# Second attention of a two-layer block: V as the stationary operand in 32-column windows, scores in two parts, loads issued a stage earlier

## The reference

```
q = (x @ wq).reshape(b, s, 32, 16)      # and k, v
q = rotary(q); k = rotary(k)
scores = einsum('bqhd,bkhd->bhqk', q, k) / 4
scores = where(causal, scores, min)
probs = softmax(scores)                 # over 256 keys
out = einsum('bhqk,bkhd->bqhd', probs, v).reshape(b, s, 512)
x = x + ga * (out @ wo)
# then: layernorm, base and router of the feed-forward, LoRA, sum
```

## Time and profile before

| | us |
|---|---|
| median of 3 runs | 2289.11 (2288.36 to 2294.61) |
| the profiled execution | 2288.56 |
| its span | 2286.5 |
| PE busy | 2075.5 (91%) |
| DVE busy | 1523.6 (67%) |
| ACT busy | 867.3 (38%) |
| POOL busy | 843.6 (37%) |

### The profile page before, as it was taken

How to read it: one execution, slowest core, us unless ns; L and a number is a source line. 1 busy time by engine, 2 the same in 40 slices (tenths; PEclk the granted TensorE clock), 3 DMA queues, 4 the chain that set the end, 5 groups by cost and what they waited for, 6 DMA issues and landing times. The chain is left out here.

```text
span 2286.5 us, 41946 instructions
## 1 busy us (share of the span) xinstructions
PE 2075.5 (91%) x13536; PEld 1830.8 (80%) x13536; DVE 1523.6 (67%) x2334; ACT 867.3 (38%) x2214; POOL 843.6 (37%) x789
## 2 busy tenths in 40 slices
PE   7789977999999999999999999669969999996873
PEld 3178867999999999999999999559958999995762
DVE  1446656787787787787787787478833444443885
ACT  1022223444444444444444444244523444433321
POOL 0012325444444444444444433258632222220224
PEclk9889998999999999999999999879988999997997
DMA  4546751111111111111111111236563222210003
GB/s 155 180 156 214 242 197 60 55 42 41 55 41 42 55 41 45 51 41 46 51 41 46 48 30 32 72 107 191 161 173 101 77 76 76 75 50 30 29 23 115
DMA packets 189217, 192.30 MB, mean 84 GB/s; under 512 B 18008, under 2 KB 167128, under 8 KB 188152
## 3 DMA queue, kind: packets, MB, share of 16 engines
q1 hardware_dynamic: 189176, 191.77, 26.9%
HBM read 120.33 MB, written 62.98 MB: 80 GB/s over the span
## 5 line engine op out<-in xcount | busy, mean ns | idle before, releaser
L836 PE MATMUL ps_q<-ht_hi,wq 128*128 (+1 forms) x2048 | 288.3, 284 | 18.2 <-DVE wq L759 18.2
L836 PEld LDWEIGHTS ps_q<-ht_hi,wq 128*128 128x128 f32 x2048 | 269.1, 192 | 23.6 <-DVE wq L759 18.4
L663 ACT ACTIVATE prob<-ps_s,neg_max 128x128 f32<-128x128 f32 (+1 forms) x512 | 208.6, 420 | 142.9 <-DVE neg_max L739 118.8
L798 POOL TENSOR_TENSOR q_rot<-q_rot,q_swap 128x512 f32<-128x512 f32 x128 | 165.4, 1292 | 197.9 <-DVE q_swap L732 197.9
L670 ACT ACTIVATE pt<-ps_s 128x512 fp32r<-128x512 f32 x192 | 108.2, 600 | 308.8 <-PE ps_s L887 308.8
L875 PE MATMUL ps_y<-wo,ot 128*128 (+1 forms) x780 | 198.1, 402 | 0.0
L875 PE MATMUL ps_o<-wo,ot 128*128 (+1 forms) x780 | 193.7, 397 | 0.2
L1690 POOL TENSOR_SCALAR_AFFINE_SELECT f_prob<-f_prob 128x512 f32<-128x512 f32 x128 | 81.6, 637 | 281.5 <-ACT f_prob L1672 281.5
L1741 PE MATMUL f_ps_o<-values,f_prob 128*128 (+1 forms) x1536 | 182.8, 276 | 0.7 <-DVE o L1645 0.7
L1741 PEld LDWEIGHTS f_ps_o<-values,f_prob 128*128 128x128 f32 x1536 | 178.8, 193 | 0.9 <-issue 0.9
L793 POOL TENSOR_TENSOR prob<-prob,inv_sum 128x512 f32<-128x512 f32 x64 | 66.7, 1042 | 296.2 <-DVE inv_sum L748 296.2
(11 more groups left out here) (235 smaller groups left out, 4490.8 us busy)
## 6 DMA issues: line engine op xcount, KB each, us to landing
stack_dram<-e_part SPq DMA_DIRECT2D x192, 128.0 KB, 2.3
v_dram<-v_part SPq DMA_DIRECT2D x32, 512.0 KB, 5.9
k_dram<-k_part SPq DMA_DIRECT2D x64, 256.0 KB, 2.7
kk<-k_dram SPq DMA_DIRECT2D x128, 128.0 KB, 2.1
vv<-v_dram SPq DMA_DIRECT2D x128, 128.0 KB, 2.1
wmod<-in_wmod SPq DMA_DIRECT2D x12, 1024.0 KB, 5.5
f_q<-stack_dram SPq DMA_DIRECT2D x64, 192.0 KB, 2.6
f_k<-stack_dram SPq DMA_DIRECT2D x128, 96.0 KB, 2.5
```

The costliest lines, as they stand in the source:

```text
L663: nc.scalar.activation(p[:, h], sc[:, h], ACT.Exp, bias=neg_max[:, t, h:h + 1], accum_out=row_sum[:, t, h:h + 1]).then_inc(p_exp, 1)
L798: nc.gpsimd.tensor_tensor(qrot[j][:], qrot[j][:], qswap[j][:], ALU.add).then_inc(q_add, 1)
L836: mm = nc.tensor.matmul(ps_q[j][:, e], w[:, c:c + HD0], r[:, bass.ds(u % B, 1), k].rearrange("p o s -> p (o s)"), start=(n == 0), stop=(n ...
```

## The change

**Attention.** V is loaded from memory as `f_v` tiles for two units: for each unit, key tile and head a window of 32 columns, in which the 16 columns of V stand at 0 to 15 or 16 to 31, by the unit's parity, and zeros elsewhere. The window is the stationary operand and P streams (`values`, line 1798 now). Head h writes partitions 32h to 32h+31; two units fill one tile of [128, 2, 256]: the products, and beside them the sums, made by the same products with `ones` as stationary operand. Everything is accumulated in one group over both units. The result has features on the partitions, so nothing is turned in the router stage; the rows of wo are permuted on the host to fit. DVE takes one reciprocal and one product for two units, behind the maxima. The scores are made in two parts, t=1 ahead of `shifted` and t=0 behind it, each with a semaphore step of its own. 16 products whose result isn't used (`warm`) run once, before the first `values`.

**Projections.** ACT writes V to a staging tile and SP stores it to memory (`store_values`). The k tiles' constants are loaded and copied at the stage's start. In the last step SP loads the first four units and two V tiles before the last q stores, and the last k stores are issued by ACT.

```diff
+                def store_values(b):
+                    sp.wait_ge(v_out, 2 * b + 4)
+                    sp.dma_start(keep.values1[bass.ds(b, 1)].rearrange("o m p x -> p (o m) x"), stage_pairs).then_inc(v_kept, 16)
...
-                    store(b, 0)
+                    if b == B - 1:
+                        sp.wait_ge(own_out, SLOTS)
+                        sp.wait_ge(v_kept, 32)
+                        for n in range(2):
+                            sp.wait_ge(qk_out[n], 192)
+                        for u in range(SLOTS):
+                            load_unit(sp, keep, u, u)
+                        for i in range(2):
+                            load_values1(sp, keep, i, i)
+                    store(sp, b, 0)
...
-                    store(b, 1)
+                    if b < B - 1:
+                        store(sp, b, 1)
+                    store_values(b)
...
                     act.wait_ge(p_done, 6 * b + 5 + t)
+                    act.wait_ge(v_kept, 16 * b + 16)
...
+def load_values1(sp, keep, w, i):
+
+    src = keep.values1[bass.ds(w // KT, 1), bass.ds(w % KT, 1)].rearrange("o m p x -> p (o m x)")
+    sp.dma_start(keep.v1[i][:], src).then_inc(keep.v1_in[i], 16)
...
+                    for t, sc in ((1, s1), (0, s0)):
+                        dve.wait_ge(s_done, 2 * u + 2 - t)
+                        nc.vector.tensor_reduce(neg_max[first][:, t], sc, AX, ALU.max, negate=True).then_inc(smax, 1)
...
+                def output(w, i):
+
+                    dve.wait_ge(o_done, 2 * w + 2)
+                    nc.vector.reciprocal(inv_sum[i][:], ps_o[i][:, 1]).then_inc(o_rcp, 1)
+                    dve.wait_ge(o_rcp, w + 1)
+                    dst = keep.ot1[:, bass.ds(w, 1)].rearrange("p o s -> p (o s)")
+                    nc.vector.tensor_tensor(dst, ps_o[i][:, 0], inv_sum[i][:], ALU.mult).then_inc(o_out, 1)
...
+                def warm():
+
+                    for n in range(WARM):
+                        nc.tensor.matmul(ps_o[1][:], q[3][0:2 * ROWS, 0, 0:P], k[3][0:2 * ROWS, 0:2], start=True, stop=True,
+                                         skip_group_check=True)
...
+                    for half in range(2):
+                        for p, c, cols in ((prob0[par], 0, slice(0, S)), (prob1[par], 1, slice(P, S))):
+                            for h in range(HU):
+                                at = par * V_UNIT + (c * HU + h) * V_WIN
+                                lhs = ones[:, par] if half else v[i][:, at:at + V_WIN]
+                                mm = nc.tensor.matmul(ps_o[i][h * V_WIN:(h + 1) * V_WIN, half, cols], lhs, p[:, h],
+                                                      start=not (par or half or c), stop=bool(par and half and c), skip_group_check=True)
...
                     if -1 <= at < U - 1:
                         turn_max(v + 1, (slot + 1) % 2, at)
+                    if at < U - 2:
+                        scores(v + 2, (slot + 2) % NS, at, 1)
                     if 0 <= at < U:
                         shifted(v, slot, at)
                     if at < U - 2:
-                        scores(v + 2, (slot + 2) % NS, at)
+                        scores(v + 2, (slot + 2) % NS, at, 0)
+                    if at == 1:
+                        warm()
                     if 1 <= at:
-                        values(v - 1, (slot + 1) % 2, at)
-
+                        values(v - 1, (slot - 1) % NS)
...
                def step(b, turned):
                     output(b + 1)
-                    if turned:
-                        pe.wait_ge(norm.ready, KT * b + KT)
-                        turn_o(b + 2)
```

More of the change, by code:

```diff
@@ L44 @@
 STACKED = ((0, 1, 0), (0, 0, 1))
-V_COLS = 112
+V_WIN = 32
+V_UNIT = TT * 4 * V_WIN
+HU1 = 4
+SLOTS = 4
 THETA = 10000.0
@@ L1140, in steps, with store @@
                 step(b, b % 2)
+        def store(engine, b, n):
+            for c in range(2):
+                engine.wait_ge(p_lo, 4 * b + 2 * n + c + 4)
+                for j, i in enumerate(STACKED[n]):
+                    for g in range(2):
+                        dst = keep.stacks1[n][bass.ds(b, 1), 16 * g:16 * g + 16, j, 8 * c:8 * c + 8]
+                        engine.dma_start(dst.rearrange("o h d s -> (o h) d s"),
+                                         f32(parts[n][c][i][:, g])).then_inc(qk_out[n], 16)
         with nc.Block() as block:
@@ L1562, in sem @@
             return ctx.enter_context(nc.semaphore(name))
[L1564 to L1566 removed]
+        q, k, v = keep.q1, keep.k1, keep.v1
+        qk_in, v_in = keep.qk1_in, keep.v1_in
         neg_max = [sb(f"f_neg_max{s}", [P, TT, HU]) for s in range(2)]
@@ L1624, in _, with step @@
                 sp.dma_start(keep.g_rl[:, :, NR:], io["a1"]).then_inc(g_raw_in, 16)
-                with sp.Fori(1, U // NS) as n:
+                def step(n, more):
                     for j in range(NS):
                         sp.wait_ge(t_done, 2 * (NS * n + j - NS) + 2)
-                        load(NS * n + j, j)
+                        load_unit(sp, keep, NS * n + j, j)
+                        if j == 0 and more:
+                            sp.wait_ge(o_done, NS * n - 4)
+                            load_values1(sp, keep, 2 * n - 1, 1)
+                        if j == 2:
+                            sp.wait_ge(o_done, NS * n - 2)
+                            load_values1(sp, keep, 2 * n, 0)
+                step(1, False)
+                with sp.Fori(2, U // NS) as n:
+                    step(n, True)
+                sp.wait_ge(o_done, U - 4)
+                load_values1(sp, keep, PAIRS - 1, 1)
                 sp.wait_ge(g_raw_in, 64)
@@ L1633, in maxima @@
                 def maxima(u, first):
[L1634 to L1645, removed]
+                    for t, sc in ((1, s1), (0, s0)):
[7 more added lines that the diff above has]
+                    nc.vector.tensor_tensor(dst, ps_o[i][:, 0], inv_sum[i][:], ALU.mult).then_inc(o_out, 1)
                 def step(v, slot, at):
-                    if 2 <= at:
-                        output(v - 2)
                     if at < U - 2:
                         maxima(v + 2, slot % 2)
-                dve.wait_ge(own_in, 16)
-                for tile in k:
-                    nc.vector.tensor_copy(tile[:], own[:]).then_inc(own_out, 1)
+                    if 2 <= at and slot % 2:
+                        output((v - 3) // 2, (slot + 1) // 2 % 2)
+                dve.sem_inc(o_out, 2)
+                for par in range(2):
+                    nc.vector.memset(ones[:, par, HD1 * (1 - par):HD1 * (2 - par)], 0.0).then_inc(ones_out, 1)
+                    nc.vector.memset(ones[:, par, HD1 * par:HD1 * (par + 1)], 1.0).then_inc(ones_out, 1)
                 steps(dve, step)
-                output(U - 1)
+                output(PAIRS - 1, 1)
             @block.scalar
```

146 lines of the change are left out of this document (64 added, 82 removed).

## The result

| | before | after |
|---|---|---|
| median, us | 2290.41 (2288.36 to 2294.61, 4 runs) | 2212.01 (2210.92 to 2215.3, 4 runs) |
| ratio, 95% interval | | 0.9658 (0.964 to 0.9676) |
| profiled execution; span | 2288.56; 2286.5 | 2215.3; 2213.6 |
| period of the second attention | 5.18 | 4.00 |

What follows compares the result with a forecast made beforehand. TensorE bounds the second attention, DVE the router stage. Terms -54 - 2 - 2.5 - 2 + 3 - 2.7 = -60 from 2288.56 give 2228.6, 2229 as median; range 2200 to 2298, the sum's own range 2204 to 2260.

Steps and rivals of the forecast that it cites:

- What bounds the kernel: Second attention: TensorE (PE) alone sets the pace, period 5.18 us a unit; router stage: DVE sets it.
- Values: Attention's products of P and V: 2.67 to 1.76 us a unit with four bands, -54 us in all; chance 0.48.
- issue price of 0.072 us a pair: Values: product plus weight load, from a row of 8-column products; 32 pairs cost 2.3 us a unit.
- Two halves in a line: Rival, values: waiting instructions block those behind, so values take 2.56 to 2.7 us; 2285 us, chance 0.30.
- bands one after the other: Rival, values: one moving stream whatever the bands, values 5.12 us a unit; 2437 us, chance 0.16.
- the clock: Rival, attention: narrow-band products don't hold the clock up, periods cost about 1.6 us more; about 2380 us, chance 0.06.
- New order: Attention: second tile's scores and reduction go first; cost nothing, or 0.1 to 0.3 us a unit if the loop bound.
- loop of 3.7: Attention's scores, reductions and turned maxima: next turning possible at about 3.7 us, below the 4.27 period, so not binding.
- First loads: Between projections and attention: earlier copies and loads start PE at 1707 to 1710 against 1711.1; -2.5 us, between -7 and +4.
- forecast of the end by bytes: Last stores and early loads: 7.3 MB at 290 to 333 GB/s take 22 to 25 us, to 1706 to 1709.
- Ramp: Attention's first steps: split scores -2 us; 16 warming products +3, between 0 and +6.
- Tail and router stage: Attention's tail -2 us; router's start -2.7, between -5 and +1, as copies and turnings go; router's steady part unchanged.

Runs made afterwards that it cites:

- e3: Changed kernel with all value products of one head issued before the next head's, instead of interleaved: 2339.39 us, ratio 1.023 to the kernel before.
- e1: Changed kernel with all four heads writing the same 32 PSUM partitions, so one band, and warming products writing both result tiles in turn: 2458.85 us.
- e2: Changed kernel with heads 0 and 2 in one band, 1 and 3 in another, and warming products writing both result tiles in turn: 2291.18 us.
- e4: Changed kernel without the row-sum products, warming products writing both result tiles in turn: 2187.05 us, ratio 0.9563 to the kernel before.
- e5: Changed kernel with the scores of both tiles behind the transposed ones, as before the change: 2212.54 us, ratio 0.9665 to the kernel before.
- e7: Changed kernel without the reciprocal, the product taking a tile of ones instead: 2207.91 us, ratio 0.9648 to the kernel before.
- e6: Changed kernel with the division of two units ahead of its step's two reductions instead of behind them: 2219.38 us, ratio 0.9703 to the kernel before.
- e11: Changed kernel with the loads of the first four units and two V tiles back at the attention's start: 2210.94 us, ratio 0.9668 to the kernel before.
- e8: Kernel before with only the new order, scores in two parts and second tile's reduction first: 2281.84 us against 2289.29 beside it, ratio 0.9973.
- e9: Changed kernel without the 16 warming products: 2202.84 us, ratio 0.9633 to the kernel before.

## Why the prediction was right

**What bounds the kernel** was read right: PE set the pace at full clock before and does after.

**Values.** Mechanism right, size off. The step was "1.76 us, halfway between 1.28 and this second price": it took 1.43. No row stood behind the halfway point, so that the forecast came as near as it did is in part luck. The issue price of 0.072 us a pair belonged to loads of 128 columns and did not bound 32-column ones. The period came out 0.27 us under the forecast 4.27 (the rest of it took 2.57 instead of 2.51), and 60 times 0.27 are 16 of the 17 us by which the forecast was too slow. Four bands gave 5.12/1.43 = 3.6 times.

**Rivals.** "Two halves in a line" falls by the 1.43 us of the changed kernel and by e3, "bands one after the other" by e1 and e2 (it is the truth for one band: 2459 against my 2437), "the clock" by the row of 1.00.

**New order.** "Cost nothing" was right, but its loop of 3.7 is 3.41 in truth (e4), and the order was not needed (e5). The division was bounded at 0.69 us an instruction by the nearest rows: 1.75 and 0.42. The term held because the division lay behind the maxima, in DVE's idle time (e7); ahead of them it would have cost 7 us (e6).

**First loads.** -2.5 predicted, -1.3 measured. PE's start at 1707.40 lies inside 1707 to 1710, but 2.3 of the 3.7 us by which it came earlier are the scatter of the projections' end. The forecast of the end by bytes held; that the loads themselves gain is wrong (e11).

**Ramp.** "-2" for the split was 4.0 (e8), shorter first values brought 2.6 (22.28 to 19.69, e8 to e9), "+3" for warming was +5.4: together -1.3 against my +1. That the sum is near is luck: the first was half of what it measured, the second wasn't in the sum, and the third was too small.

**Tail and router stage.** -2 and -2.7 predicted, -3.4 measured to the router's first output product. Whether something was lost or won behind it can't be told from the scatter of 6 us. The steady part is DVE's as before, busy 64 of 72 us (2061 to 2133), and an element takes 18.3 us on the mean of seven where it took 18.2.

The sum by measured terms: -71.1 - 1.3 - 1.3 - 3.4 = -77, against a difference of medians of 78. The upper end of the sum's own range should read 2264, not 2260: 2288.56 less 25.

## What to carry to other kernels

Where the result has few columns, give TensorE's products disjoint 32-column bands and interleave them head by head: price the group by the busiest band's columns plus about 0.15 us, and don't let more than a few instructions in a row go to one band (eight in a row cost 2 us a unit here). Measure warming before keeping it: products at half clock cost double. Once TensorE's piece shrinks, look at what the masks, sums and divisions are for; dropping a mask that only a softmax shift needed gave 27 us more, for inputs on which the shift can't underflow a row.

## What was not expected of the hardware

- TensorE starts an instruction for a free band ahead of three earlier ones that wait for a busy band, and not ahead of four (e3: order and depth read from the recorded starts; what makes the limit isn't shown).
- A weight load of 32 columns and a float32 instruction of 128 or 256 columns pass in 45 ns on average over four bands (1.43 us for 32). That is what the bands stream, not a price of issue: four heads' first instructions start within 0.04 us (1875.00 to 1875.04).
- DVE's reciprocal takes 1.75 us for 256 elements of a partition and 0.21 for 8, so 6.2 ns for each further element. A product of 256 takes 0.42 us, a reduction of 512 elements 0.69 and of 1024 1.22.
